# Softmax denominators of a graph attention layer on TensorE, with a column of ones, instead of a running sum on GpSimd

## What is computed

```
e     = leaky_relu(a_src[src] + a_dst[dst], 0.2)
e     = exp(e - segment_max(e, dst))
s     = segment_sum(e, dst)                   # the denominators
out   = segment_sum(h[src] * (e / s[dst]), dst)
```

## Time and profile before

| | us |
|---|---|
| median of 3 runs | 4486.59 (4484.09 to 4494.87) |
| span of the profiled execution | 4488.1 |
| TensorE busy, whole span | 3479.2 (78%) |
| GpSimd busy, whole span | 821.0 (18%) |
| g2, first weight matmul to reciprocals of the last head | 1804.63 to 2086.66 |
| g3, first weight matmul to the end of the last pass | 2429.29 to about 2574.8 |

### The profile page before, as it was taken

The page is one execution under the profiler, slowest core; times in us unless marked ns, Lnnn a source line. Parts: engine busy times, 40 slices in busy tenths (PEclk is TensorE's granted clock), DMA queues, the critical chain, the costliest instruction groups (busy, mean ns, idle before and its releaser), DMA issues. The chain is left out here.

```text
span 4488.1 us, 53210 instructions
## 1 busy us (share of the span) xinstructions
PE 3479.2 (78%) x19962; PEld 3212.7 (72%) x19963; DVE 2280.6 (51%) x3552; ACT 1404.6 (31%) x1882; POOL 821.0 (18%) x626
## 2 busy tenths in 40 slices
PE   8715577667879686775686918999978999969999
PEld 7715466557769585554685707888868999969998
DVE  6736677475423466897666684233223233222332
ACT  2203344242333233432233412222223323323233
POOL 0000244140000031443232002112102122010210
PEclk9956789568879798988798959999988999979999
DMA  0020000003121220000210032121112121121311
GB/s 2 18 107 28 4 1 4 5 22 101 53 69 46 98 75 13 1 0 34 79 44 4 1 110 75 43 71 51 62 59 77 61 84 48 43 99 40 108 54 63
DMA packets 103611, 219.10 MB, mean 49 GB/s; under 512 B 8884, under 2 KB 83073, under 8 KB 101198
## 3 DMA queue, kind: packets, MB, share of 16 engines
q1 hardware_dynamic: 103448, 217.01, 14.3%
HBM read 171.13 MB, written 45.85 MB: 48 GB/s over the span
## 5 line engine op out<-in xcount | busy, mean ns | idle before, releaser
L1414 PE MATMUL psum<-v,g_wgt 125*125 125x256 f32 (+2 forms) x2600 | 564.0, 381 | 180.9 <-DVE g_wgt L1282 167.9
L1414 PEld LDWEIGHTS psum<-v,g_wgt 125*125 125x125 f32 x2600 | 490.3, 211 | 252.4 <-DVE g_wgt L1282 193.0
L847 POOL CAST p_w_hi<-p_w_raw 128x384 fp32r<-128x384 f32 (+3 forms) x248 | 179.1, 722 | 2610.8 <-DMA p_w_raw<-in_L_gnn_w_rel_dram 1293.6
L946 DVE TENSOR_TENSOR p_l_lo<-h_t,p_l_hi 128x750 fp32r<-128x750 f32 (+2 forms) x440 | 482.1, 1102 | 226.3 <-ACT p_l_hi L893 221.6
L1064 PE MATMUL psum<-p_w_hi,p_l_lo 128*125 128x384 f32 (+4 forms) x2844 | 550.5, 333 | 34.4 <-DVE p_l_lo L946 33.5
L1064 PE MATMUL psum<-p_w_lo,p_l_hi 128*125 128x384 f32 (+4 forms) x2844 | 541.2, 330 | 0.0
L1064 PE MATMUL psum<-p_w_hi,p_l_hi 128*125 128x384 f32 (+4 forms) x2844 | 537.9, 328 | 0.0
L893 ACT CAST p_l_hi<-h_t 128x750 fp32r<-128x750 f32 (+2 forms) x440 | 390.9, 893 | 404.5 <-PE psum L1064 331.9
L1064 PEld LDWEIGHTS psum<-p_w_hi,p_l_lo 128*125 128x125 f32 (+1 forms) x2844 | 473.1, 192 | 57.6 <-DVE p_l_lo L946 46.7
L1064 PEld LDWEIGHTS psum<-p_w_lo,p_l_hi 128*125 128x125 f32 (+1 forms) x2844 | 475.0, 192 | 9.2
L1064 PEld LDWEIGHTS psum<-p_w_hi,p_l_hi 128*125 128x125 f32 (+1 forms) x2844 | 472.5, 190 | 9.4
(11 more groups left out here) (174 smaller groups left out, 3879.4 us busy)
## 6 DMA issues: line engine op xcount, KB each, us to landing
p_c<-c_dram SPq DMA_DIRECT2D x18, 3051.8 KB
p_w_raw<-in_L_gnn_w_rel_dram SPq DMA_DIRECT2D x78, 192.0 KB
p_w_raw<-in_L_gnn_w_rel_dram SPq DMA_DIRECT2D x42, 224.0 KB
c_dram<-counts SPq DMA_DIRECT2D x3, 3051.8 KB
res_dram<-p_fin SPq DMA_DIRECT2D x70, 125.0 KB
x_dram<-p_fin SPq DMA_DIRECT2D x40, 187.5 KB
t_rows<-x_dram SPq DMA_DIRECT2D x20, 375.0 KB
act_dram<-p_fin SPq DMA_DIRECT2D x40, 187.5 KB
```

The lines of the kernel that those rows point to most:

```text
L847: pool.tensor_copy(w_hi[0:rows, j % 2, b, :width(j)], raw).then_inc(hi_made, 1)
L946: dve.tensor_tensor(l_lo[0:rows, t % 2, b:b + cnt], src[0:rows, q:q + cnt, t * P:(t + 1) * P], l_hi[0:rows, t % 2, b:b + cnt].bitcast(F32) ...
L1414: ins = pe.matmul(acc(t), w[:, t * P:(t + 1) * P], v[:, b, h, c:c + wide], start=(b == 0 and first), stop=(b == NT - 1), skip_group_check= ...
```

## The change

GpSimd's part of g2 and g3 is taken out, with the buffer `wsum` and both semaphores. In the first pass of each head every weight matmul is followed by one with the same piece of the weight tile as stationary operand and a column of ones streaming past it, which accumulates the denominators in PSUM bank `DEN` (bank 5) over the ten blocks. VectorE's waits on GpSimd and on the separate denominator matmuls go away; it reads the denominators once the pass's last matmul is done.

```diff
-        wsum = None if ones_col else sb("wsum", [P, N], F32)
...
-                else:
-                    for p, (h, c) in enumerate(passes):
-                        if not new_head(p):
-                            continue
-                        if h:
-
-                            pool.wait_ge(den_done, h)
-                        for b in range(NT):
-                            m = NT * p + b
-                            pool.wait_ge(weighed, m + 1)
-                            if b == 0:
-                                pool.tensor_copy(wsum[:], wgt[:, m % NW]).then_inc(summed, 1)
-                            else:
-                                pool.wait_ge(summed, NT * h + b)
-                                pool.tensor_tensor(wsum[:], wsum[:], wgt[:, m % NW], ALU.add).then_inc(summed, 1)
...
                         dve.wait_ge(wgt_used, m - NW + 1)
-                        if not ones_col:
-                            q, r = divmod(m - NW, NT)
-                            hq = passes[q][0]
-                            dve.wait_ge(summed, NT * hq + (r + 1 if new_head(q) else NT))
...
                     elif new_head(p):
-                        dve.wait_ge(den_done, h + 1)
                         step(dve.reciprocal(rden[:], ps[0:P, DEN, 0:NT]))
...
                         ins = pe.matmul(acc(t), w[:, t * P:(t + 1) * P], v[:, b, h, c:c + wide],
                                         start=(b == 0 and first), stop=(b == NT - 1), skip_group_check=True)
+                        if not ones_col and new_head(p):
+                            ins = pe.matmul(ps[0:P, DEN, t:t + 1], w[:, t * P:(t + 1) * P], k.ones[0:P, 0:1],
+                                            start=(b == 0 and t == 0), stop=(b == NT - 1), skip_group_check=True)
                     ins.then_inc(wgt_used, 1)
...
-                    if not ones_col and new_head(p):
-                        pe.wait_ge(summed, NT * (h + 1))
-                        for t in range(NT):
-                            ins = pe.matmul(ps[0:P, DEN, t:t + 1], wsum[:, t * P:(t + 1) * P], k.ones[0:P, 0:1],
-                                            start=(t == 0), stop=True, skip_group_check=True)
-                        ins.then_inc(den_done, 1)
```

More of the change, by code:

```diff
@@ L1176, in attention @@
         wgt_used = sem("wgt_used")
-        summed = sem("summed")
-        den_done = sem("den_done")
         acc_read = sem("acc_read")
```

## The result

The changed kernel is slower: 4615.88 us median against 4490.73, ratio 1.028 with a 95% interval of 1.022 to 1.034. The median stands for no run, though. The four runs are 4643.7, 4643.8, 4584.0 and 4588.0 us, two values 58 us apart. The profiled execution is one of the first kind.

What follows compares the result with a forecast made beforehand. VectorE, stretched by GpSimd's addition, often set attention's pace; TensorE would bind afterwards. Terms 6.9 + 2 + 74.4 + 77.7 = 161 us on 4488.1 gave 4649 us; range 4632 to 4672, with the full-clock last-head rival 4570 to 4672.

Steps and rivals of the forecast that it cites:

- case A: Main forecast: g2's last head and g3's first pass both stay at half clock; 4649 us, chance 0.55.
- Case B: Rival: g2's last head keeps full clock, only g3's first pass is slow; 4584 us, chance 0.22.
- Head 3: g2's last head: +10.8 us at full clock, +74.4 if the clock falls at its start.
- Removed: g2 and g3's first pass: GpSimd's 50 instructions, VectorE's stretching (1.7 us or more a block), five separate denominators, 2.24 us each.
- Case D: Rival: bare loads are hidden and VectorE's relief shows; -53 us, 4434 us, chance 0.04.
- Added: 500 one-column f32 matmuls, 20 pairs a block; two bare loads of 0.109 us per tile, 2.14 us a block.
- Full clock: At full clock: g2 heads with preparation 73.25 us, last head 64.9, g3's first pass 66.2.
- Case C: Rival: the clock rises in the new stream as in the old; +23 us, 4509 us, chance 0.13.
- The clock: g2 and g3's first pass: the new stream keeps its starting clock until row makers lift it; half clock adds 6.46 us a block.
- g3's first pass: Starts at half clock with no row maker, so ten slow blocks: +77.7 us.
- Head 0: g2's first head: block 0 and half the row maker slow, 81.2 us against 74.4, +6.9.
- heads 1 and 2: g2's middle heads: -3.0 and -4.1 us at full clock, 0.65 chance of a 7.1 us clock fall each; together +2.

Runs made afterwards that it cites:

- e3: Changed kernel without the inline one-column matmuls; ten separate ones with a constant operand at each head's end, so denominators are constant: 4430.8 us, ratio 0.986.
- e7: Changed kernel with the weight tile written in fp32r and the ones' matmuls (two columns) made in fp32r, one load instead of two: 4457.5 us, ratio 0.9925.
- e9: Changed kernel with long filler matmuls in TensorE's waits, plus a second, unused one-column matmul behind each first: 4615.6 us.
- e1: Changed kernel with 51 columns of ones in place of one behind each weight tile: 4511.1 us, ratio 1.0045.
- e11: Changed kernel with shortened filler: 8 extra matmuls before block 0 of g2 and g3, 1 at each g2 head boundary: 4501.4 us, ratio 1.0029.
- e2: Changed kernel with each block's ten one-column matmuls moved behind its ten long ones, same instructions: 4533.4 us.
- e4: Changed kernel plus unused 500-column matmuls in TensorE's waits: 14 before block 0 of g2 and g3, 3 at each g2 head boundary: 4509.9 us.
- e5: Changed kernel with 3 extra matmuls at each boundary between g2's heads, none at a stage's start: 4574.5 us median.

## Why the prediction was right

The forecast was 4649 us, of case A; the two runs of that case gave 4643.7 and 4643.8. Case B was 4584 us; the other two gave 4584.0 and 4588.0. Head 3 lost the clock in two of four runs (seen in the profiled one, inferred for the others), where 0.55 had been given to A and 0.22 to B. The median of four, 4615.9, is a mean of the two kinds and no forecast of mine; it lies within the range for any split, since the range was drawn around both.

- *Removed.* VectorE's stretching went as forecast, all its long instructions at 1.46 us. By e3 the relief is 59 us. Case D's sum had given 53 with no denominator matmuls at all, while e3 still has five times 2.24 us of them, so the relief was put too small by some 17 us. A part of that is the block with preparation, 5.94 us where 6.18 was added up: the second `largest` gives way after 1.39 us, and 1.61 was taken for both. Nothing of case A rests on it, since TensorE bound every block.
- *Added.* The tile was put at 0.646 us (a block at 6.46) and is 0.65; the 0.109 us for a bare load is what a short pair costs in e7 and e9. A slow block, put at 12.9, is 12.7 to 12.8.
- *Full clock.* Case C was 4509 us. e1, with the clock up, gave 4511; e11 gave 4501, with the slow starts gone too, which C had counted at 2.3 us each.
- *The clock.* The step that carried the result, that this stream would keep the clock it starts with, was read from streams with 192 and 97 columns. It held in g3's first pass, in head 3, and until each row maker; e1, e2 and e4 show that the clock and what streams between the loads are the cause, each by another way (more streaming, another order, another start). The page "TensorE: Matmul & The Clock Gate" of the Trainium skill ("Why this matters for your kernels") says to keep TensorE continuously busy to get the full clock; case C was made by that rule. The trace does not agree: TensorE was busy 126 of 127 us in head 3 and stayed at 1.2 GHz, and the measurement decides.
- *Sizes that were off.* g3's first pass +75.7 for +77.7 and head 3 +72.9 for +74.4, both since a slow block is 12.7 and not 12.9. Head 0 +7.9 for +6.9: its first row maker ran at 1.2 GHz from end to end (4.51 us for 2.35), where half of it had been taken. With heads 1 and 2, together 0.0 for +2 (one fell and one held, where 0.65 had been taken for each), the stages give 156.5 us for 161. The span rose 153.8; the 2.7 us between are not placed.

What stays open is what sets whether the clock falls behind a boundary. The idle time is 1.3 us at all of them, the two falls came about 0.6 us after TensorE had started again, and one of three held in the profiled run. With the filler of e5 there was no fall at any of them, in the profiled run by its clock and in the others, so far as their times tell.

## What to carry to other kernels

Price a matmul with few columns by its weight load, and ask which matmul hides each load: in every form tried here each short matmul left one load bare. Then ask what the new mixture does to the clock: a stream paced by loads can run at half clock for its whole length with TensorE never idle, so look for such a stream in the old trace, and give short matmuls columns to stream, even useless ones, when they fit in the load's shadow. A helper engine that nobody waits for may still cost time, through the engine that it slows; test it by leaving its work out.

## What the runs showed that was not expected

- The clock of the kernel before fell inside its heads as well, in eight blocks of g2 (see e3). The prediction had looked for falls at the boundaries alone.
- Executions of one program differ by 58 us. By inference, it is whether the clock fell once, just behind a boundary with 1.3 us of idle time.
- 51 columns in place of one cost no time at all in the tile (0.65 us) and are worth 70 to 130 us by the clock. e1's expectation forecast this; the prediction had no such form.
- e9, with half of its time in bare loads, kept a granted clock of 1.00 from 2530 to 2600 us, in g3's first pass, where no row maker helps; its expectation had left open that it would fall. So a stream that keeps the clock need not be able to lift it: the changed kernel's own stream kept 1.00 through that pass in e4 (72 us) and stayed at 0.50 through it without the filler.
